# One stage of a four-layer graph network: the clearing of the sums' banks moves from TensorE to ScalarE, and registers are loaded for four groups at a time

## The reference, cut to what matters

```python
h = x @ w_in + b_in                                   # 6250 x 64
Wij = (ssp(f_ij @ w_f1 + b_f1) @ w_f2 + b_f2) * rcut_ij[:, None]
x_ij = h[idx_j] * Wij                                 # one row of 64 per edge
agg = jax.ops.segment_sum(x_ij, idx_i, num_segments=n_atoms)   # idx_i = source node
```

## Time and profile before

| what | value |
|---|---|
| median of 3 runs | 6109.31 us (6107.77 to 6119.23) |
| the profiled execution's own time | 6114.9 us |
| its span | 6113.6 us |
| granted TensorE clock, mean over the span | 0.731 |
| busy share: PE, DVE, ACT, POOL | 57%, 58%, 27%, 64% |
| the stage in question | 1606 us to 1902 us of the span |

### The profile page before, as it was taken

One profiled execution on the slowest core, in us unless ns is written; L12 is line 12 of the kernel. 1 busy time (PEld: TensorE's weight loads), 2 busy tenths in 40 slices (PEclk: granted clock), 3 DMA queues, 4 the chain that ended last, 5 costly groups with the idle time before them and its releaser, 6 DMA issues. The chain is left out here.

```text
span 6113.6 us, 101731 instructions
## 1 busy us (share of the span) xinstructions
PE 3505.3 (57%) x21281; PEld 2677.6 (44%) x21282; DVE 3544.8 (58%) x8298; ACT 1658.3 (27%) x4002; POOL 3885.4 (64%) x3879
## 2 busy tenths in 40 slices
PE   7758888888697333333354444444226645555666
PEld 5646666666575333333342222222126633434444
DVE  9858888888697343334364444444464454444444
ACT  7635555555344000000020000000037721111112
POOL 0047777777662677777717777777425527777774
PEclk9968999999898555555575555555569968877667
DMA  3069999999563212112138888888847622222221
GB/s 91 4 178 275 283 281 279 283 278 282 148 157 79 55 52 52 52 52 52 50 108 273 274 266 268 268 268 267 185 119 202 198 66 58 58 58 58 58 58 53
DMA packets 937029, 939.40 MB, mean 154 GB/s; under 512 B 330232, under 2 KB 777930, under 8 KB 936842
## 3 DMA queue, kind: packets, MB, share of 16 engines
q1 hardware_dynamic: 770906, 549.05, 33.5%
q0 software_dynamic: 137776, 369.86, 18.7%
q10 hardware_dynamic: 28288, 19.84, 1.1%
HBM read 686.22 MB, written 252.06 MB: 153 GB/s over the span
## 5 line engine op out<-in xcount | busy, mean ns | idle before, releaser
L1593 POOL DMA_INDIRECT edges_kv<-kv,edges_idx x880 | 922.4, 1048 | 399.6 <-issue 264.9
L963 POOL DMA_INDIRECT by_src<-edges_rows,edges_pos x832 | 903.4, 1086 | 263.0 <-issue 258.0
L2205 POOL DMA_INDIRECT sum_rows<-table,sum_idx x832 | 807.0, 970 | 348.3 <-issue 253.3
L1322 POOL DMA_INDIRECT sum_rows<-table,sum_idx x832 | 790.2, 950 | 362.0 <-issue 251.5
L1399 PE MATMUL sum_p_sum<-sum_hot,sum_rows 128*128 128x128 f32 x1664 | 387.6, 427 | 665.6 <-DMA sum_rows<-table,sum_idx 665.6
L1399 PEld LDWEIGHTS sum_p_sum<-sum_hot,sum_rows 128*128 128x128 f32 x1664 | 359.8, 328 | 693.5 <-issue 693.5
L2303 PE MATMUL sum_p_sum<-sum_hot,sum_msg 128*128 128x128 f32 x1664 | 373.8, 416 | 464.4 <-DVE a_acc L2264 458.0
L1674 DVE TENSOR_TENSOR edges_kv<-edges_kv,edges_ekv 128x1024 f32<-128x1024 f32 x220 | 260.2, 1224 | 627.4 <-DMA edges_kv<-kv,edges_idx 627.4
L2303 PEld LDWEIGHTS sum_p_sum<-sum_hot,sum_msg 128*128 128x128 f32 x1664 | 349.1, 319 | 550.0 <-issue 550.0
L1378 DVE TENSOR_TENSOR a_acc<-a_acc,sum_p_sum 128x128 f32 x832 | 235.6, 283 | 547.4 <-PE sum_p_sum L1399 546.3
L735 PE MATMUL edges_p_attr<-k_wekv,edges_attr 128*128 128x256 f32 x1664 | 476.8, 436 | 98.8 <-ACT edges_rows L810 98.5
(11 more groups left out here) (379 smaller groups left out, 7665.7 us busy)
## 6 DMA issues: line engine op xcount, KB each, us to landing
edges_ekv<-by_src SPq DMA_DIRECT2D x110, 1024.0 KB
v<-edges_kv SPq DMA_DIRECT2D x110, 512.0 KB, 4.0
sum_vv<-v SPq DMA_DIRECT2D x110, 512.0 KB, 4.0
edges_attr<-in_attr128T SPq DMA_DIRECT2D x104, 512.0 KB
edges_near<-h_in SPq DMA_DIRECT2D x832, 48.0 KB
sum_rows<-by_src SPq DMA_DIRECT2D x110, 264.0 KB, 3.0
edges_src_b<-rel SPq DMA_DIRECT2D x110, 256.0 KB
edges_dst_b<-dst SPq DMA_DIRECT2D x104, 256.0 KB
```

The costliest lines, as they stand in the source:

```text
L963: nc.gpsimd.indirect_dma_start(Dr.by_src0, bass.IndirectOffsetOnAxis(pos[:, q, j:j + 1], 0), rows[:, q % 2, j, :], None).then_inc(scattere ...
L1322: nc.gpsimd.indirect_dma_start(rows[:, q, j, :], None, Dr.table, bass.IndirectOffsetOnAxis(idx[:, q, j:j + 1], 0)).then_inc(fetched[q], 16)
L1593: nc.gpsimd.indirect_dma_start(kv[:, q, j, :], None, Dr.kv, bass.IndirectOffsetOnAxis(idx[:, q, j:j + 1], 0)).then_inc(fetched[q], 16)
L2205: nc.gpsimd.indirect_dma_start(rows[:, q, j, :], None, Dr.table, bass.IndirectOffsetOnAxis(idx[:, q, j:j + 1], 0)).then_inc(fetched[q], 16)
```

## The change

ACT clears both banks with one copy of a 64 x 1024 tile of zeros (`wipe`), for group g + 2 as soon as the add of group g is done, ahead of `keep` of the same group; PE's two matmuls of zeros go, and PE waits for the new semaphore `wiped` in place of `added`. PE loads the slots of four groups (32 values) with one load at the head of each turn of its loop, and DVE the first blocks of four groups (4 values, 8 apart) likewise.

```diff
-    none16 = s.sb("none16", [1, 512], BF16)
+    none = s.sb("none", [F0, GE])
...
+            def wipe(h):
+
+                nc.scalar.copy(p_sum[:, h].rearrange("p j n -> p (j n)"), none[:]).then_inc(wiped, 1)
...
-            with nc.scalar.Fori(0, NG2 // L) as i:
-                for q in range(L):
-                    keep(i * L + q, q, i + 1)
...
+            act.wait_ge(cleared, 1)
+            for g in range(2):
+                wipe(g)
+                keep(g, g, 1)
+            full = (NG2 - 2) // L
+            with nc.scalar.Fori(0, full) as i:
+                for q in range(L):
+                    act.wait_ge(added, i * L + q + 3)
+                    wipe(q % 2)
+                    keep(i * L + q + 2, (q + 2) % L, i + 1 + (q + 2) // L)
...
-            nc.vector.memset(none16[:], 0.0).then_inc(cleared, 1)
+            nc.vector.memset(none[:], 0.0).then_inc(cleared, 1)
...
-            def add(g, q):
-
-                first = load_values(nc, DVE, K.srt_blk[0:1, bass.ds(g * G, 1)], NB)
+            def block_at(g, n):
+
+                return load_values(nc, DVE, K.srt_blk[0:1, :].rearrange("a (g j) -> a g j", j=G)[:, bass.ds(g, n), 0], NB)
...
             with nc.vector.Fori(0, full) as i:
+                at = block_at(i * L, L)
                 for q in range(L):
-                    add(i * L + q, q)
+                    add(i * L + q, q, at[q])
                     hots(i * L + q + 2, (q + 2) % L)
...
-            pe.wait_ge(cleared, 1)
-            def sums(g, q, loads):
+            def slots_of(g, n):
+
+                at = load_values(nc, PE, K.srt_slot[0:1, bass.ds(g * G, n * G)], G - 1)
+                return [at[k * G:(k + 1) * G] for k in range(n)]
+
+            def sums(g, q, loads, slot):
...
-                slot = load_values(nc, PE, K.srt_slot[0:1, bass.ds(g * G, G)], G - 1)
                 pe.wait_ge(hot_ready, g + 1)
-                pe.wait_ge(added, g + 1)
-                for b in range(2):
-                    nc.tensor.matmul(p_sum[:, h, 4 * b:4 * b + 4, :].rearrange("p j n -> p (j n)"), none16[0:1, 0:F0], none16[0:1, :], start=True, stop=False, skip_group_check=True)
+                pe.wait_ge(wiped, g + 1)
...
             with nc.tensor.Fori(0, NG2 // L) as i:
-                for q in range(L):
-                    sums(i * L + q, q, i + 1)
+                slots = slots_of(i * L, L)
+                for q in range(L):
+                    sums(i * L + q, q, i + 1, slots[q])
```

## The result

The kernel after took 6188.1 us (median; 6181.2 to 6191.8), the kernel before 6111.4 on the same chip (6107.8 to 6119.2): a ratio of 1.0123, interval 1.0105 to 1.0140. The forecast was 6138, slower by 29; it came out slower by 77, outside the range. The span of the profiled execution grew from 6113.6 to 6190.3 us. By the starts of the stages, `sum_by_source` went from 295.9 to 382.7 us (+86.8) and the rest of the program lost 10.1.

What follows compares the result with a forecast made beforehand. It took a lap of PE and DVE over two groups to bound `sum_by_source`; afterwards PE's load would set the turn: 28.3 for 26 turns, 0.6 for the last, 0.4 for edges, +29 us on 6109.3, 6138; range 6104 to 6166.

Steps and rivals of the forecast that it cites:

- ACT's lap: ACT's serial group of wipe, copy and DMA issue in `sum_by_source`: 2.63 us, 10.87 a turn; alone +16 us, chance 0.25.
- the wipe: ACT's copy of zeros into the banks: 1.01 us for 1024 elements, taken from rows of smaller copies.
- DVE's load: DVE's one load of four places per turn: 0.97 us, with 0.43 and 1.23 as ends.
- its cover: DVE's load of four places hidden until the one-hots end: 1.5 us hidden, so no cost.
- the memset: DVE's memset of zeros ahead of everything, grown from 256 to 1024 words: +0.6 us, between 0 and +0.9.
- the absence of a gain from PE's lost zeros: Zeros leaving PE's path could win 20 us over 27 turns, but ACT's pace and PE's load stand against it.
- 9.80 plus the load: Chain of four groups through PE's load: 11.38 us a turn at 1.58; sets the turn above a load of 1.07.
- 0.041 a value and 1.58 us for 32: Length of PE's joined load, from 0.307 us for one value and 0.592 for eight; ends 0.59 and 2.37.
- The row of three values at 0.747: Register load elsewhere at 0.22 us a value; used for DVE's load, and cited for a longer PE load.
- load long: Rival: PE's load takes 2.37 us, as four loads of eight; 12.17 a turn, +50 us, 6159; chance 0.12.
- the clock: Rival: PE idles longer, the clock falls, sums take 3.27 us instead of 1.96; +51 us, 6161; chance 0.04.
- a mean share of busy time: Argument against a clock fall: a later stage with PE 68% busy keeps 1.00; this one would have 70%.

Runs made afterwards that it cites:

- e1: Kernel before with only the wipe moved to ACT; PE and DVE still load per group: stage 309.1 us, ratio 1.0002.
- e9: Kernel after plus ten filler matmuls of ones over 128 rows in PE's gap each turn: stage 346.1 us, ratio to before 1.0049.
- e11: Kernel after plus ten filler matmuls of zeros over 128 rows in PE's gap each turn: stage 344.9 us, one run.
- e3: Kernel before with the wipe on ACT and PE loading 16 slots per two groups, DVE one place per group: stage 317.5 us, ratio 1.0020.
- e7: Kernel before with only DVE's load of four places joined, PE's code unchanged: stage 298.9 us, ratio 1.0001.
- e4: As e1 (wipe on ACT, loads per group), but SP issues the DMA storing `hot8`: stage 287.8 us, ratio to before 0.9980.
- e8: As e4, with PE's loop turning every eight groups instead of four: stage 284.2 us, ratio to before 0.9975.
- e10: Kernel after with PE's load of 32 split into four loads of 8, all at the turn's head: stage 381.8 us, ratio to before 1.0067.
- e6: Kernel before with four semaphore instructions added to PE's queue at the stage's head, outside the loop: stage 295.4 us, ratio 0.9986.

## Why the prediction was wrong

**Right in kind.** ACT's lap (2.63 forecast, 2.67 and 2.59 measured; 10.87 a turn, 10.77 in e1), the wipe (1.01), DVE's load (0.97, 0.956) and its cover, the memset (+0.6 forecast, 0.912 us with 0.272 before: +0.64), the absence of a gain from PE's lost zeros. The mechanism that decides was named too: one step in four long, the load behind the last address instruction. Its chain, "9.80 plus the load" for four groups, gives 9.80 + 2.33 = 12.13 us with the load's measured length; with the clock held up (e9) the turn was 12.15.

**Wrong: the length of the load.** The term "0.041 a value and 1.58 us for 32" drew a line through one value on DVE's queue and eight on PE's. PE's own lengths at 8, 16 and 32 (0.59, 1.32, 2.30 to 2.37) don't lie on it. The row of three values at 0.747, that I set aside for PE, was right for DVE: 0.307 + 3 x 0.216 = 0.955 is the load of four. I had the true value as the rival "load long" (2.37 us, 12.17 a turn, +50 us for 12 in 100); the measured stage without the clock's fall is 346.1 - 295.9 = +50.2.

**Wrong: the clock, and that it adds.** It had 0.04 and was worked out as a case of its own, with all sums at half clock. In the run it came on top of the long load and by way of it: the load opens a gap of 2.50 us in PE, and after it the clock falls. That the gap is the cause, and not the load, the filled gaps show (e9 and e11 against the kernel after). My argument against this rival, a mean share of busy time (68% at 1.00 in a later stage), averaged over a gap that the forecast itself had made: 3.73 us from sums to sums in one step of four is 1.8 us idle at once, and 2.5 with the long load. The Trainium skill (TensorE: Matmul & The Clock Gate, the section on HAM oscillation) says that a wait of PE in each round of a loop can throttle it each time; this case's trace agrees, with the sums behind the gap at half clock in 25 turns of 27 and 0.88 over the stage, though the waits of the section's example are longer than the 2.50 us here. The forecast's own load of 1.58 us was not run; in e3, with 1.32 us of load at two places, the clock stayed up but for 1.7 us.

**Not foreseen:** 10.1 us less outside the stage, of which 5.8 in `weighted_sums`, 2.4 in `sum_by_target` and 2.4 in `sum_messages`. The last two are shorter by as much in e7, which touches neither them nor PE's code, so they are not the change's work; the remainder lies in stages that move by some us between any two executions.

The whole: +13.2 for the wipe on ACT, +37.0 more when PE's load is 2.33 us in one piece (346.1 - 309.1), +36.6 for the clock, together +86.8; -10.1 elsewhere; +76.7 of the span. The range's upper end, 6166, held the long load or the clock, and not both.

## What to carry to other kernels

Here joining loads that were hidden saved nothing and made one piece longer than its cover; ask first how far the engine's queue runs ahead at that place, and keep the loads spread. A rival that lengthens a gap and one that depends on gaps are not exclusive: work out their sum. Before work is given to an engine with idle time, take out what its own queue waits for; here the wipe paid only once the DMA's issue had left ScalarE.

## What the runs showed of the hardware

- A register load on PE's queue took 0.59 us for 8 consecutive values (0.77 and 0.80 in e4 and e8), 1.32 for 16 and 2.30 to 2.37 for 32; on DVE's, for values 8 apart, 0.307 for one, 0.52 for two and 0.956 for four. Four loads of 8 in a row held PE's queue for 2.99 us (e10).
- Matmuls over one row, of zeros or of ones, did not keep the granted clock up through the gap (0.88 in the stage); the same over 128 rows did (1.00), even of zeros.
- With the split loads (e10) the clock stayed up through some of the gaps, one of 3.06 us among them, and was at half for longer in others; in sum it was 87 us, as in the kernel after.
- Four more instructions ahead of it made a later PE loop 0.24 us a turn faster (e6).
